# Where a fused cross-attention kernel runs its context normalisation steps and issues its loads

## The chip, the cores and the metric

One core of a Trainium2 chip. The metric is the device time of one execution in microseconds; three runs of the kernel before gave 1990.89, 1991.17 and 1993.92 us.

## The reference, cut to what matters

Cross-attention with 8 batches, 512 queries, 512 context rows, 1024 channels and 16 heads of 64 channels. Only the context is layer-normalised.

```python
a = layer_norm(ctx) * gamma + beta          # (8, 512, 1024)
Q = x @ Wq.T;  K = a @ Wk.T;  V = a @ Wv.T  # 16 heads of 64
p = softmax(where(mask, Q @ K.T * 64**-0.5, -inf))
y = x + tanh(gate) * ((p @ V) @ Wo.T)
```

## The kernel before, in words

Everything is computed on transposed tiles: 128 channels on the partitions, 512 queries or context rows along the free axis. A *body* k (0 to 63) handles one pair of heads of one batch b = k // 8, j = k % 8; the program is unrolled, and "body j" or "(b, j)" names one. "(j, h)" in the tables is body j, half h. In one body TensorE does, for each half h (one head): the scores of head h (L412, L413), the values of the head before (L432, L433), the output projection of pair k-2 (out_step, L438 to L442), and between them, dealt out by `FILL`, the 72 matmuls of the projections of pair k+1 in the order WQ, WK, WV (L485 to L489). Every operand is split into a high and a low part, so each product takes three matmuls (two for scores and values). A plain body has 132 matmuls, four of them the transposes of V (turn_v, L421).

The other engines follow their own written order; each one issues strictly in order, and semaphores join them:

- VectorE (DVE): block_maxima (L847), group_maxima (L853), key_maxima (L859), spread_maxima (L864), subtract (L869), v_low (L891), o_add (L909), column_sums (L875), accumulate (L914, the output into xy), then q_low (L897), the same chain for the other half, inverse_sums (L880 to L886), accumulate, k_low (L902), o_add and column_sums. In batch 0 norm_quarter (L968) normalises a quarter of the next context; in later batches only its statistics are taken here. o_add(k, 0) waits until GpSimd's o_scale(k-1) has read o32 (om_done). TensorE's second scores wait for both accumulates of the first half, its WK for v_low, its WV for q_low, and out_step for subtract.
- ScalarE (ACT): copy_vt (L647), o_high (L702), gather_maxima (L637) and hand_out_maxima (L642), which wait for VectorE, o_move (L681), exp (L657), v_high (L652), p_high (L662), q_high (L668, L669), which waits for the scores of its half, and k_high (L675, L676). In body 6 of a batch (kind "prepare" in batch 0, "ready" in batches 1 to 6) it also makes x_high (L714) and the eight gamma and beta steps a_float (L723) of the next context; in body 7 ("switch") a_high (L731).
- GpSimd (POOL): p_low (L1147), o_low (L1162), key_sums (L1151, L1153), o_scale (L1158); in batch 0 the splits of the weights (L1142); x_low (L1184) in body 6 and a_low (L1189) in body 7. In batches 1 to 6 it also normalises the next context, which is loaded again, transposed: `turned` (L1169 to L1179) adds the row vector of minus the means ("centre") and multiplies by the row vector of inverse deviations ("scale"), quarter by quarter. `TURNED_NORM` says in which body and half; in the first half that is ahead of o_scale and p_low(1, 0). "centre" waits for its quarter (turned_ld) and for the row vectors of its pair of quarters (row_in).
- SyncE (SP) issues all DMAs, and waits, in order. In a body of batches 1 to 6: load_kept(WV), exchange_sums (the softmax sums through HBM, L241 to L245), WQ, WK, WO, mask, store_y, the next context (load_ctx), the transposed context (load_turned, L259), spread_rows, and x. load_kept waits until TensorE has finished with the weights in place: with WQ's in the first half of a body, with WK's in the second, with WO's and WV's at its end.

spread_rows(b, pair) turns the means and inverse deviations, which stand one per partition, into row vectors: four DMAs of 128 elements of 4 bytes write them to HBM (L268), SyncE waits until all have landed, and two DMAs read them back, broadcast to all partitions (L271), into w_raw.

## Time and profile before

| | |
|---|---|
| three runs, us | 1990.89, 1991.17, 1993.92 |
| profiled execution, us | 1995.22 |
| its span, us | 1993.4 |
| granted TensorE clock, mean share | 0.996 |
| PE busy, us | 1941.4 (97%) |
| DVE busy, us | 1618.6 (81%) |
| POOL busy, us | 1573.6 (79%) |
| ACT busy, us | 1284.8 (64%) |
| DMA moved, MB | 356.67 (mean 179 GB/s) |

The profiled execution is one more run, with the profiler on. Times in the views count from the start of the span. "[2.52 <-DVE m_four L853]" behind an instruction means that its engine idled 2.52 us before it and that this instruction ended the wait; two or more of a kind in a row are merged, with their number and the time from the first's start to the last's end. A window gives its length, then for each engine the busy time and the number of instructions (PE, PEld, DVE, ACT, POOL), the share of the full TensorE clock that was granted, the share of time that the DMA engines were busy, and GB/s; its sum line adds up several windows.

### The profile page before, as it was taken

The numbers are of one execution on the slowest core, as the hardware profiler recorded it, in microseconds if no ns is written. First come the engines' busy times: TensorE is split into PE (matmuls) and PEld (weight loads), VectorE is DVE, ScalarE is ACT, GpSimd is POOL, SyncE is SP. The second block draws the span as 40 slices with busy tenths as digits, with TensorE's granted clock in tenths as the row PEclk, the third lists the DMA queues.
The fourth block names the chain that finished last, engine by engine and source line by source line (L and its number), as shares of the span: only waits on it lengthen the run. The fifth ranks groups of instructions, "written<-read, shape, count | busy, mean of one in ns | idle before, by whom it ended". The sixth has DMA issues, their size and how long they took to land.

```text
span 1993.4 us, 26143 instructions
## 1 busy us (share of the span) xinstructions
PE 1941.4 (97%) x8528; PEld 1570.1 (79%) x8528; DVE 1618.6 (81%) x2089; ACT 1284.8 (64%) x2375; POOL 1573.6 (79%) x851
## 2 busy tenths in 40 slices
PE   6999999999999999999999999999999999999997
PEld 5777778887788777888788887888778888788886
DVE  7688878887788777888788887888778888778878
ACT  5767776567656576655865668665686566756554
POOL 3899997789867888678876789768897688966664
PEclk9999999999999999999999999999999999999999
DMA  7577545664365543664446553555534655435422
GB/s 265 180 246 254 180 158 188 207 218 159 122 216 179 196 175 111 232 203 167 153 149 216 186 204 121 182 198 186 203 124 156 234 161 191 150 129 191 155 103 107
DMA packets 150039, 356.67 MB, mean 179 GB/s; under 512 B 63504, under 2 KB 67600, under 8 KB 149008
## 3 DMA queue, kind: packets, MB, share of 16 engines
q1 hardware_dynamic: 149904, 354.99, 51.4%
q8 instruction: 70, 1.15, 0.2%
q14 instruction: 65, 0.53, 0.1%
HBM read 303.54 MB, written 51.39 MB: 178 GB/s over the span
## 4 chain that ended last, share of the span: by engine, by line
PE 65%; ACT 8%; POOL 8%; DVE 7%; DMA 6%; issue 3%; SPq 2%; POOLq 0%; ACTq 0%; DVEq 0%
PE pj L485 12%; PE pj L487 12%; PE pj L489 12%; PE sc L438 4%; PE sc L442 4%; PE sc L439 4%; PE pv L432 4%; PE sc L412 4%; PE sc L413 4%; PE pv L433 4%; POOL a_lo L1189 4%; DVE mq L847 3%; DMA rows<-rstd 2%; POOL p_lo L1147 2%; ACT prob L657 2%
## 5 line engine op out<-in xcount | busy, mean ns | idle before, releaser
L1147 POOL TENSOR_TENSOR p_lo<-prob,p_hi 128x1024 fp32r<-128x1024 f32 x256 | 613.7, 2409 | 151.3 <-ACT p_hi L662 151.3
L485 PE MATMUL pj<-a_hi,w_hi 128*128 128x512 f32 x1024 | 403.9, 394 | 10.3 <-DVE qt L897 3.2
L489 PE MATMUL pj<-a_hi,w_lo 128*128 128x512 f32 x1024 | 401.4, 392 | 0.0
L487 PE MATMUL pj<-a_lo,w_hi 128*128 128x512 f32 x1024 | 401.1, 392 | 0.0
L847 DVE TRANSPOSE_TENSOR_REDUCE mq<-sc 128x32 f32<-128x1024 f32 x256 | 303.7, 1224 | 72.6 <-PE sc L413 71.7
L657 ACT ACTIVATE prob<-prob 128x1024 f32<-128x1024 f32 x256 | 271.6, 1061 | 101.2 <-DVE prob L869 100.8
L914 DVE SCALAR_TENSOR_TENSOR xy<-sc,tg_b,xy 128x1024 f32<-128x1024 f32 x244 | 304.7, 1272 | 15.0 <-PE sc L442 8.9
L869 DVE TENSOR_TENSOR prob<-sc,m_b 128x1024 f32<-128x1024 f32 x256 | 301.5, 1219 | 4.4
L1151 POOL TENSOR_TENSOR prob<-prob 128x1024 f32<-128x1024 f32 x126 | 302.5, 2401 | 0.0
L662 ACT CAST p_hi<-prob 128x1024 fp32r<-128x1024 f32 x256 | 269.3, 1052 | 3.5
L485 PEld LDWEIGHTS pj<-a_hi,w_hi 128*128 128x128 f32 x1024 | 193.1, 189 | 60.3 <-issue 6.1
L1158 POOL TENSOR_TENSOR r_b<-o,r_b 128x512 f32<-128x512 f32 x62 | 81.1, 1308 | 191.5 <-DVE r_b L886 191.5
L489 PEld LDWEIGHTS pj<-a_hi,w_lo 128*128 128x128 f32 x1024 | 193.1, 189 | 41.6
L487 PEld LDWEIGHTS pj<-a_lo,w_hi 128*128 128x128 f32 x1024 | 193.1, 189 | 40.5
L485 PE MATMUL pj<-x_hi,w_hi 128*128 128x512 f32 x512 | 208.0, 406 | 15.2 <-DVE x_lo L926 8.5
L668 ACT CAST qt<-pj 64x512 fp32r<-64x512 f32 x128 | 74.3, 580 | 220.4 <-PE sc L413 192.8
L412 PE MATMUL sc<-qt,kt 128*128 128x512 f32 x512 | 200.9, 392 | 5.5 <-DVE prob L869 3.4
L438 PE MATMUL sc<-o_hi,w_hi 128*128 128x512 f32 x494 | 197.8, 400 | 8.3 <-DVE prob L869 8.0
L432 PE MATMUL pv<-p_hi,v_st 128*128 128x512 f32 x512 | 200.5, 392 | 3.8 <-POOL p_lo L1147 3.7
L489 PE MATMUL pj<-x_hi,w_lo 128*128 128x512 f32 x512 | 202.0, 395 | 0.0
L487 PE MATMUL pj<-x_lo,w_hi 128*128 128x512 f32 x512 | 201.8, 394 | 0.0
L413 PE MATMUL sc<-qt,kt 128*128 128x512 f32 x512 | 200.1, 391 | 0.0
(129 smaller groups left out, 3735.5 us busy)
## 6 DMA issues: line engine op xcount, KB each, us to landing
w_hi<-kept_hi SPq DMA_DIRECT2D x224, 512.0 KB, 3.7
w_lo<-kept_lo SPq DMA_DIRECT2D x224, 512.0 KB, 4.7
xy<-in_xT SPq DMA_DIRECT2D x32, 512.0 KB, 6.2
cx<-in_ctx SPq DMA_DIRECT2D x32, 512.0 KB, 8.3
kept_hi<-w_hi SPq DMA_DIRECT2D x32, 512.0 KB, 5.4
kept_lo<-w_lo SPq DMA_DIRECT2D x32, 512.0 KB, 6.1
out_y<-xy SPq DMA_DIRECT2D x7, 2048.0 KB, 9.8
cx<-in_ctxT SPq DMA_DIRECT2D x24, 512.0 KB, 7.3
```

The source lines that it names most:

```text
L412: pe.matmul(sc[:, s], kt[:, h, 0, cols], qt[:, h, 0], start=True, stop=False)
L413: mm = pe.matmul(sc[:, s], kt[:, h, 1, cols], qt[:, h, 1], start=False, stop=True)
L432: pe.matmul(pv[h][:, 0], w, p_hi[:, s], start=s == 0, stop=False)
L485: pe.matmul(dst, w_hi[:, w, cols], s_hi[:, i], start=i == 0, stop=False)
L487: pe.matmul(dst, w_hi[:, w, cols], s_lo[:, i], start=False, stop=False)
L489: mm = pe.matmul(dst, w_lo[:, w, cols], s_hi[:, i], start=False, stop=i == KT - 1)
L657: act.activation(p, p, ACT.Exp, scale=SCALE).then_inc(exp_done, 1)
L847: dve.tensor_reduce(out=mq[:, 2 * i:2 * i + 2], in_=sc[:, 2 * i:2 * i + 2].rearrange("p s (b j) -> p s b j", j=32), op=ALU.max, axis=mybir ...
L869: dve.tensor_tensor(prob[:, h, 2 * i:2 * i + 2], sc[:, 2 * i:2 * i + 2], m_b[:].rearrange("p (o t) -> p o t", o=1).to_broadcast((P, 2, T)) ...
L914: dve.scalar_tensor_tensor(out=y, in0=sc[:, 2 * where:2 * where + 2], scalar=tg_b[:, bass.ds(parity, 1)], in1=y, op0=ALU.mult, op1=ALU.add ...
L1147: pool.tensor_tensor(p_lo[:, 2 * i:2 * i + 2], prob[:, h, 2 * i:2 * i + 2], f32(p_hi[:, 2 * i:2 * i + 2]), ALU.subtract).then_inc(pl_done, 1)
L1151: pool.tensor_tensor(prob[:, h, 0:2], prob[:, h, 0:2], prob[:, h, 2:4], ALU.add).then_inc(sum_done, 1)
```

## The change

- SyncE, batches 1 to 6: spread_rows of pairs 0 and 1 moves from bodies 2 and 3 to bodies 3 and 4, directly behind exchange_sums; the mask, context, transposed context and x loads move from the end of the body's list to in front of WQ's load. On GpSimd the uses of the row vectors stay where they are but for centre 3, which goes from (5, 0) to (4, 1).
- ScalarE, body 6 of batches 1 to 6: the eight a_float go from four pairs among the exponentials to three at the body's start, four between q_high(k, 0) and q_high(k, 1), and one at its end. TensorE's wait for all of them at the start of body 7 is left out in those batches (it guards PSUM banks that only batch 0's steps read).
- Bodies 0 and 1 of batch 0: v_high and v_low go ahead of the exponentials and of subtract.
- Body 5 of batch 0: norm_quarter goes from in front of key_maxima to behind subtract.

```diff
--- before.py
+++ after.py
@@ -49,8 +49,9 @@
 
 
 TURNED_LOADS = {2: 0, 3: 1}
+SPREAD_ROWS = {3: 0, 4: 1}
 TURNED_NORM = {(3, 0): (("centre", 0), ("scale", 0)), (3, 1): (("centre", 1),), (4, 0): (("scale", 1), ("centre", 2)),
-               (4, 1): (("scale", 2),), (5, 0): (("centre", 3), ("scale", 3))}
+               (4, 1): (("scale", 2), ("centre", 3)), (5, 0): (("scale", 3),)}
 
 
 FILL = ((5, 4, 7, 2, 18), (5, 4, 9, 2, 16))
@@ -334,23 +335,24 @@
                         keep_split(NUMBER[WO, PAIRS - 1])
                     load_kept(WV, (j + 1) % PAIRS, k)
                     exchange_sums(k - 1)
+                    if j in SPREAD_ROWS:
+                        spread_rows(b, SPREAD_ROWS[j])
+                    if j == 0:
+                        next_mask(b)
+                    for s in CTX_LOADS[1].get(j, ()):
+                        load_ctx(b, s)
+                    if j in TURNED_LOADS:
+                        load_turned(b, TURNED_LOADS[j])
+                    if 2 <= j <= 5:
+                        load_x(b, j - 2)
                     load_kept(WQ, (j + 2) % PAIRS, k)
                     load_kept(WK, (j + 2) % PAIRS, k)
                     if k == PAIRS + 1:
                         sp.wait_ge(w_out[WO], 32 * PAIRS)
                     if k > PAIRS:
                         load_kept(WO, (j - 1) % PAIRS, k)
-                    if j == 0:
-                        next_mask(b)
                     if j == 1:
                         store_y(b - 1, k)
-                    for s in CTX_LOADS[1].get(j, ()):
-                        load_ctx(b, s)
-                    if j in TURNED_LOADS:
-                        load_turned(b, TURNED_LOADS[j])
-                        spread_rows(b, TURNED_LOADS[j])
-                    if 2 <= j <= 5:
-                        load_x(b, j - 2)
 
             def last_batch():
                 b = B - 1
@@ -513,7 +515,7 @@
                 stream = projections(k, b, kind)
                 for h in range(2):
                     f = FILL[h]
-                    if kind == "switch" and h == 0:
+                    if kind == "switch" and h == 0 and b == 0:
                         pe.wait_ge(at_done, b * KT + 2 * KT)
                     if kind == "prepare" and h == 1:
                         pe.wait_ge(at_done, b * KT + (KT + 4))
@@ -738,11 +740,16 @@
                 if begun and splits(*out_split(k)):
                     ge(act, op_done, k * 4 - 8)
                     split_w(*out_split(k))
+                if kind == "ready":
+                    for i in range(3):
+                        a_float(b, i)
                 if kind == "switch":
                     for i in range(KT // 2):
                         a_high(k, b, i)
                 gather_maxima(k, 0)
                 hand_out_maxima(k, 0)
+                if k < 2:
+                    v_high(k)
                 if kind == "switch":
                     for i in range(KT // 2, KT):
                         a_high(k, b, i)
@@ -753,17 +760,21 @@
                 if begun:
                     o_move(k - 1, 1)
                 exp(k, 0, 0)
-                v_high(k)
+                if k >= 2:
+                    v_high(k)
                 p_high(k, 0, 0)
                 exp(k, 0, 1)
-                if kind in ("prepare", "ready"):
+                if kind == "prepare":
                     a_float(b, 0)
                     a_float(b, 1)
                 p_high(k, 0, 1)
-                if kind in ("prepare", "ready"):
+                if kind == "prepare":
                     a_float(b, 2)
                     a_float(b, 3)
                 q_high(k, 0)
+                if kind == "ready":
+                    for i in range(3, KT - 1):
+                        a_float(b, i)
                 q_high(k, 1)
                 if (j, 0) in MOMENTS[b > 0] and b < B - 1:
                     moments(b, MOMENTS[b > 0][j, 0])
@@ -782,15 +793,17 @@
                 exp(k, 1, 0)
                 k_high(k, 0)
                 p_high(k, 1, 0)
-                if kind in ("prepare", "ready"):
+                if kind == "prepare":
                     a_float(b, 4)
                     a_float(b, 5)
                 exp(k, 1, 1)
-                if kind in ("prepare", "ready"):
+                if kind == "prepare":
                     a_float(b, 6)
                     a_float(b, 7)
                 k_high(k, 1)
                 p_high(k, 1, 1)
+                if kind == "ready":
+                    a_float(b, KT - 1)
 
             def last_body(k):
                 copy_vt(k)
@@ -974,15 +987,20 @@
                 block_maxima(k, 0, 0)
                 block_maxima(k, 0, 1)
                 group_maxima(k, 0)
-                if b == 0 and (j, 0) in NORM:
+                if b == 0 and j == 6:
                     norm_quarter(NORM[j, 0])
                 key_maxima(k, 0)
                 spread_maxima(k, 0)
+                if k < 2:
+                    v_low(k)
                 subtract(k, 0, 0)
                 subtract(k, 0, 1)
+                if b == 0 and j == 5:
+                    norm_quarter(NORM[j, 0])
                 if kind == "prepare":
                     accumulate(k, 0, 0, 0, 0, b % 2)
-                v_low(k)
+                if k >= 2:
+                    v_low(k)
                 if begun:
                     o_add(k - 1, 1)
                     column_sums(k - 1, 1)
```

## Rows read from the trace of the kernel before

**Rows 1.** Page: span, and section 1 (busy us, share, instructions).

```profile
span 1993.4 us, 26143 instructions
...
PE 1941.4 (97%) x8528; PEld 1570.1 (79%) x8528; DVE 1618.6 (81%) x2089; ACT 1284.8 (64%) x2375; POOL 1573.6 (79%) x851
```

**Rows 2.** Windows of bodies 6 and 7, batch 3 (columns as said above).

```profile
952.78:983.98 31.20, 30.42 (x134) 24.06 (x132) 22.64 (x28) 25.18 (x47) 28.77 (x18) 1.00 0.45 158
983.98:1016.25 32.27, 30.94 (x132) 24.23 (x133) 25.07 (x32) 25.23 (x46) 29.32 (x18) 1.00 0.38 130
```

**Rows 3.** Windows, sums over batches 1 to 6: bodies 0-3; 4-5; 6-7.

```profile
sum 712.83, PE 712.83 PEld 583.63 DVE 609.29 ACT 429.70 POOL 510.98; mean PE 118.81 PEld 97.27 DVE 101.55 ACT 71.62 POOL 85.16
...
sum 360.99, PE 358.26 PEld 291.64 DVE 296.13 ACT 212.07 POOL 318.33; mean PE 59.71 PEld 48.61 DVE 49.36 ACT 35.35 POOL 53.05
...
sum 380.88, PE 368.02 PEld 289.75 DVE 286.25 ACT 302.46 POOL 348.43; mean PE 61.34 PEld 48.29 DVE 47.71 ACT 50.41 POOL 58.07
```

**Rows 4.** Timeline of ACT, batch 3, bodies 5 (923.09) and 6 (952.78).

```profile
940.22 0.58 ACT L668 CAST qt<-pj 64x512 fp32r<-64x512 f32 x1 [3.40 <-PE sc L413]
...
952.98 0.59 ACT L647 COPY vt<-pj 128x512 f32<-128x512 f32 x1 [0.99 <-PE pj L489]
...
956.60 0.66 ACT L637 COPY m_four<-m_four 32x16 f32<-32x16 f32 x3 [2.52 <-DVE m_four L853]
...
964.47 1.51 ACT L723 ACTIVATE cx<-cx,bet,gam 128x512 f32<-128x512 f32 x2
```

**Rows 5.** Timeline of POOL, body 7 of batch 3 (983.98).

```profile
993.48 7.58 POOL L1189 TENSOR_TENSOR a_lo<-cx,a_hi 128x512 fp32r<-128x512 f32 x6
...
1003.39 2.53 POOL L1189 TENSOR_TENSOR a_lo<-cx,a_hi 128x512 fp32r<-128x512 f32 x2
```

**Rows 6.** DMA view of 1135.5 to 1149: GB/s in 40 slices.

```profile
GB/s 401 364 316 316 376 437 376 376 449 413 401 425 425 292 113 14 0 0 0 0 0 0 0 0 0 0 0 0 0 0 0 0 0 0 0 0 0 70 55 64
```

**Rows 7.** Timeline of SP: body (3, 5) from 923.09; end of (4, 3).

```profile
935.99 1.75 SPq L245 DMA_DIRECT2D r_four<-sums  x4
...
1135.66 0.43 SPq L268 DMA_DIRECT2D rows<-rstd  x1
1146.37 0.80 SPq L271 DMA_DIRECT2D w_raw<-rows  x2
```

**Rows 8.** Line 271 (the row vectors' loads), all 24 of them.

```profile
DMA to landing us min/median/max: 3.0/4.8/6.3
```

**Rows 9.** Timeline of POOL, body 3 of batch 3 (863.01).

```profile
882.38 4.91 POOL L1179 TENSOR_TENSOR cx<-cx,w_raw 128x1024 f32<-128x1024 f32 x2
...
889.33 2.42 POOL L1147 TENSOR_TENSOR p_lo<-prob,p_hi 128x1024 fp32r<-128x1024 f32 x1
```

**Rows 10.** Timelines of PE, DVE, start of body (3, 6), 952.78.

```profile
954.59 0.39 PE L485 MATMUL pj<-x_hi,w_hi 128*128 128x512 f32 x1
...
957.54 0.39 PE L432 MATMUL pv<-p_hi,v_st 128*128 128x512 f32 x1
...
952.05 0.68 DVE L909 TENSOR_TENSOR o<-pv,o_tmp 64x512 f32<-64x512 f32 x1
...
953.88 1.25 DVE L847 TRANSPOSE_TENSOR_REDUCE mq<-sc 128x32 f32<-128x1024 f32 x1 [0.53 <-PE sc L413]
```

**Rows 11.** Batch 0: windows (body 5; a slow stretch), timelines of PE, DVE.

```profile
186.42:220.37 33.95, 31.47 (x133) 25.45 (x132) 29.75 (x38) 21.81 (x39) 30.29 (x16) 0.95 0.61 204
...
51.03:54.42 3.39, 3.39 (x9) 2.61 (x10) 0.17 (x1) 3.13 (x5) 3.24 (x2) 0.53 0.87 272
...
51.03 0.60 PE L485 MATMUL pj<-a_hi,w_hi 128*128 128x512 f32 x1 [2.05 <-DVE v_st L891]
...
70.41 0.47 PE L485 MATMUL pj<-x_hi,w_hi 128*128 128x512 f32 x1 [1.20 <-ACT vt L647]
...
196.78 0.50 PE L438 MATMUL sc<-o_hi,w_hi 128*128 128x512 f32 x1 [2.48 <-DVE prob L869]
...
190.86 3.01 DVE L968 TENSOR_SCALAR cx<-cx,nmean,rstd 128x1024 f32<-128x1024 f32 x1
```

## The prediction

> **What bounds the kernel now.** The page comes first: TensorE is busy for 97% of the span with 8528 matmuls [rows 1]. So the end can move only where TensorE waits, and I cut the span at body starts (the first score matmul of a head pair) to find those places. In batch 3 body 6 takes 31.20 us and body 7 32.27 [rows 2]. Batches 1 to 6 all behave alike: their bodies 0 to 3 sum to 712.83 us, which makes an undisturbed body 29.70; bodies 4 and 5 to 360.99, 4.6 over 12 x 29.70; bodies 6 and 7 to 380.88, 24.5 over [rows 3]. Those 29.1 us, and the waits of batch 0, are all that the change can win. Below, "at 14.7" means 14.7 us after the start of the body.
>
> **Gamma steps (a_float), batches 1 to 6.** Eight ACTIVATEs a batch, about 0.71 us each back to back, sit between the exponentials and casts of body 6 [rows 4]: they delay the q casts, then VectorE's q_low, and last the k casts, so that copy_vt of body 7 starts about 2 us late. After the change three run at body start, where ScalarE idles 2.52 us before gather_maxima: 3 x 0.71 = 2.1, cover enough. Four run after q_high(0), where a plain body idles 3.40 us before q_high(1): 2.8, covered. The last goes in front of the next copy_vt, where 0.99 us is idle [rows 4]; x_high, which stays, takes 0.6 of that, so vt comes about 0.3 late, and the first WQ matmul wants it at 1.8, a full microsecond later. Body 6 falls to 29.70: 1.50 x 6 = 9.0 us. The wait on at_done, which would hold the scores of body 7 for that last step, is gone for these batches.
>
> Body 7 doesn't fall all the way. GpSimd has six a_low, p_low, two a_low, p_low in a row [rows 5]. Started from a body 6 without the late ScalarE, I get the first a_low at 7.6 instead of 9.5, the last done at 20.05, and p_low(0,1) at 22.4. TensorE wants them at 19.6 and 22.1: 0.8 us stays. Gain 2.57 - 0.8 = 1.77, times 6 = 10.6.
>
> **Loads reordered, batches 1 to 6.** No DMA is added, only SyncE's order changes. Today spread_rows comes last in bodies 2 and 3 and blocks SyncE over the body's end; V's weights for body 4 then start late and TensorE waits for them. That is the 4.6 us of bodies 4 and 5, and it goes, since V's load now has SyncE free at the body's start. In bodies 0 to 2 the context and x loads now stand ahead of WQ's. WQ is issued some 2 us later behind at most 1.5 MB; the queue moves 512 KB in about 1.3 us (400 GB/s, [rows 6]), so it lands by 25, wanted at 31.3: nothing.
>
> **What the new order costs.** spread_rows of pair 0 moves from the end of body 2 to body 3, behind exchange_sums, yet GpSimd's first use of it, turned("centre", 0), stays in (3, 0). In a plain body SyncE is through with exchange_sums at 14.7 [rows 7]. Then:
> - Four 0.5 KB DMAs are issued to about 16.2. The trace has none in a quiet queue. In one spread the last was issued at 1135.66 and SyncE went on at 1146.37 [rows 7]; the DMA engines were already idle from 1140.9 on [rows 6]. So over 5 us of it was no queueing behind bulk loads. The four land over about 5 us. Bounds: overlapping as r_four's four are issued, in 1.75 us, done at 18; or the whole 10.7 after the last issue, done at 27. I take 16.7 for the first (2 after its issue) and 5 more: 21.7, because the idle engines show the tail to be the transfer's own.
> - The two row vectors then need 3.0 to 6.3 us, median 4.8 [rows 8], the second one issued 0.4 later: ready at 21.7 + 0.4 + 4.8 = 26.9 = x (from 18 + 0.4 + 3.0 = 21.4 to, with a second late, 29).
>
> GpSimd comes to "centre" at 19.4 today, with its row in place, takes 4.91 us for centre and scale, and starts p_low(1,0) at 26.32 [rows 9]. After the change it waits to x. Then centre, scale (4.9), o_scale (1.3), p_low(1,0) and p_low(1,1) (2.35 each) end at x + 11.0. TensorE wants the last one at 4.76 - 0.2 of the next body, so at 34.25; and VectorE's o_add waits for o_scale, done at x + 6.3 against 28.96 with 0.53 us of slack behind it [rows 10]. Both give the same threshold: a stall of x - 23.3, 3.6 us. WQ of body 4 is now issued after the spread, behind two context loads and one of x: five loads of 1.3 us make it x + 6.8 = 33.7, wanted at 31.3 [rows 10]. That 2.4 us overlaps the other stall, but after idle times of 2.05 and 2.48 us the trace shows TensorE at 1.2 instead of 2.4 GHz for a few us, which adds about 0.5 here [rows 11]. Together 4.1.
>
> Pair 1 does the same in body 4: centre 2 is the second step of (4, 0), with one turned step less behind it, so the threshold is 25.8, and x = 26.9 costs 1.1. Centre 3, moved to (4, 1), gives GpSimd four steps in body 4 and one in body 5. Its backlog is worked off in body 5 (19.4 + 2.4 of 29.7 us) before x_low: nothing. Cost 5.2 x 6 = 31.2 us.
>
> **Batch 0.** In body 5 the normalisation ran 3.01 us, started as GpSimd went from one operation to the next, with key_maxima and everything of that half behind it; TensorE waited 2.48 and then ran at half clock, and the body took 33.95 [rows 11]. Moved behind subtract it costs 1.0 to 3.0 us (I take 1.85: the rest of a GpSimd operation and its own 0.56) and pushes v_low, o_add and both accumulates, for which the second scores wait: about 0.95, and 0.5 more at out_step. 4.25 - 1.45 = 2.8 gained. In bodies 0 and 1 the early V copies end TensorE's waits for v_low, 2.05 us in body 0, but the body's end hangs on ScalarE's chain, as the 1.20 us wait for vt in body 1 shows [rows 11]. v_low ahead of subtract puts 0.7 us into that chain, q_low(0) leaves it earlier only in body 0: -1.3 and +0.4, so 1.0 gained (bounds 0 and 4).
>
> **Sum.** -9.0 - 10.6 - 4.6 - 2.8 - 1.0 = -28.0, and +31.2: +3.2 us. The profiled execution took 1995.2 (span 1993.4), 4.1 above the median 1991.2 of the runs; the difference is put onto the median: 1994.4, rounded 1994. Each microsecond of x is worth 12 us, so x decides, and with it I would be within or just beyond 0.2% (4 us), about what a measurement tells from no change.
>
> **Rivals.**
> - *The rows come early.* With an empty queue the four small DMAs overlap, and x is 21 to 26. For it: no row shows them alone. Against it: the idle 5 us [rows 6]. At x = 25 the cost is 1.7 x 6 = 10, time 1973; below 23.3 none, 1963. Chance 0.22. The Trainium skill (DMA: Bandwidth & Descriptors, "Anatomy of one DMA") gives a DMA about 2.0 us fixed, most of it the write receipt. By that rule alone the last small one would land at 18.2 and the vectors at 20.9, no stall, 1963; the trace of before doesn't agree, as its small DMAs took 10.7 us.
> - *Slower: the stall feeds itself.* Its place is the hand-over from body 3 to 4. Where x passes 27.6, WQ's wait passes 3 us, half clock follows in both bodies, and the stall of body 4 passes 1.8: 6.6 us a batch at 27.6 and 7.4 at 28, so +12 to +16 us, 2003 to 2008, and more beyond. The point from which it decides is x = 27.6. For it: the longest landings [rows 8]. Chance 0.18.
> - *The gamma steps don't free body 6* because ScalarE's start idle is too short: then 9 us less is won, 2003. Body 7's wait for a_low speaks for GpSimd as the next bound, the idle rows against. Chance 0.05, with other small errors that give no change.
>
> **Numbers.** The forecast has 0.55 with x from 26.0 to 27.6, a range of its own of 1981 to 2003, of it 0.15 faster, 0.20 same, 0.20 slower. Faster 0.15 + 0.22 = 0.37; same 0.20 + 0.03 = 0.23; slower 0.20 + 0.18 + 0.02 = 0.40. The range 1966 to 2008 leaves out the stall-free end of the first rival.
>
> **What would show it.** Right: bodies 6 at 29.7 and 7 near 30.5 in batches 1 to 6; SyncE waiting some 5 us for rows<-rstd from 16 on in bodies 3 and 4; GpSimd idle before L1179's first centre; bodies 4 (whose start takes the stall) about 34, body 5 near 31; half clock after WQ's wait. Wrong: bodies 3 to 5 all at 29.7, or body 6 still over 30.5; then the landing of the small DMAs or the idle of ScalarE was misread.

## The result and the profile after

The changed kernel takes 2043.74 us (median of 4 runs, 2042.27 to 2047.24) beside 1991.03 (median of 4) for the kernel before on the same chip: a ratio of 1.0266, interval 1.0247 to 1.0285. It is 53 us slower; the forecast was 1994 with a range up to 2008. The profiled execution took 2042.95. Page of the kernel after, span, section 1, and three groups of section 5 (busy, mean ns | idle before them, releaser):

```profile
span 2041.2 us, 26143 instructions
PE 1956.4 (96%) x8528; PEld 1583.0 (78%) x8528; DVE 1617.1 (79%) x2089; ACT 1287.7 (63%) x2375; POOL 1570.1 (77%) x851
...
L487 PE MATMUL pj<-x_hi,w_hi 128*128 128x512 f32 x512 | 214.4, 419 | 59.3 <-DMA w_lo<-kept_lo 47.4
L434 PE MATMUL pv<-p_hi,v_st 128*128 128x512 f32 x512 | 207.3, 405 | 5.8 <-POOL p_lo L1165 5.5
L1197 POOL TENSOR_TENSOR cx<-cx,w_raw 128x1024 f32<-128x1024 f32 x48 | 114.6, 2394 | 117.4 <-DMA w_raw<-rows 116.9
```

TensorE waits 59 us in front of the projections, mostly for weights from a DMA; GpSimd waits 117 us for the row vectors. Windows of the kernel after, as in [rows 3]: sums over batches 1 to 6 of bodies 0-3, 4-5 and 6-7; then bodies 3 to 7 of batch 3:

```profile
sum 712.75, PE 712.75 PEld 583.33 DVE 605.88 ACT 429.64 POOL 456.55; mean PE 118.79 PEld 97.22 DVE 100.98 ACT 71.61 POOL 76.09
...
sum 434.09, PE 384.37 PEld 306.02 DVE 299.08 ACT 213.25 POOL 369.46; mean PE 64.06 PEld 51.00 DVE 49.85 ACT 35.54 POOL 61.58
...
sum 361.15, PE 359.96 PEld 291.18 DVE 287.07 ACT 303.99 POOL 348.38; mean PE 59.99 PEld 48.53 DVE 47.85 ACT 50.66 POOL 58.06
...
877.02:906.70 29.68, 29.68 (x133) 24.30 (x132) 25.29 (x34) 17.96 (x35) 15.71 (x9) 1.00 0.27 59
906.70:944.67 37.97, 31.96 (x134) 25.66 (x132) 25.12 (x34) 17.77 (x33) 28.71 (x15) 0.91 0.52 171
944.67:978.62 33.95, 31.75 (x134) 25.09 (x133) 24.75 (x32) 17.77 (x33) 32.89 (x17) 0.95 0.62 230
978.62:1008.32 29.70, 29.70 (x134) 24.30 (x133) 23.93 (x30) 27.07 (x49) 28.34 (x18) 1.00 0.42 143
1008.32:1038.80 30.48, 30.27 (x133) 24.23 (x132) 23.89 (x31) 23.60 (x44) 29.74 (x19) 1.00 0.41 141
```

So the whole loss stands in one place: bodies 4 and 5 went from 360.99 to 434.09 (+73.1), 77.7 us over 12 x 29.70 (50.6 in bodies 4, 27.1 in bodies 5), with a lower granted clock in both. Bodies 6 and 7 went from 380.88 to 361.15 (-19.7). Batch 0 in this trace is 4.5 us shorter. How the stall comes about, timelines of the kernel after in batch 3: SP in body 3 (from 877.02), POOL and PE at the start of body 4 (906.70).

```profile
889.90 1.74 SPq L246 DMA_DIRECT2D r_four<-sums  x4
891.75 0.36 SPq L269 DMA_DIRECT2D rows<-nmean  x1
...
893.11 0.43 SPq L269 DMA_DIRECT2D rows<-rstd  x1
901.04 3.22 SPq L272 DMA_DIRECT2D w_raw<-rows  x2
904.30 0.91 SPq L260 DMA_DIRECT2D cx<-in_ctxT  x2
...
905.78 0.50 SPq L229 DMA_DIRECT2D w_hi<-kept_hi  x1
...
908.28 4.76 POOL L1197 TENSOR_TENSOR cx<-cx,w_raw 128x1024 f32<-128x1024 f32 x2 [11.85 <-DMA w_raw<-rows]
...
914.69 0.79 PE L487 MATMUL pj<-x_hi,w_hi 128*128 128x512 f32 x1 [6.01 <-DMA w_lo<-kept_lo]
915.28 0.63 PE L489 MATMUL pj<-x_lo,w_hi 128*128 128x512 f32 x1
```

SyncE issues the four small DMAs from 14.73 to 16.1 us after the body's start and can go on at 24.02: 7.9 us after the last issue. In the six batches this point lies at 23.2 to 26.2, mean 24.4. The row vectors are complete at 30.2 to 31.8, mean 30.95: that is x. WQ's weights, issued at 28.76 in this body, land at 37.63 where they are wanted at 31.3. In all six bodies 4 it is WQ's low half that ends TensorE's one long wait (5.0 to 6.5 us, mean 5.8); the rest of the 8.4 us that such a body is over 29.70 follows at its restart, with 7 to 14 matmuls at half clock. Lines 269 and 272 of the kernel after, issue to landing, in their order:

```profile
DMA to landing us min/median/max: 5.6/6.7/9.6
...
DMA to landing us min/median/max: 3.1/5.4/7.7
```

Where these 7.9 us go the DMA views show, which count the packets by size; those of the small DMAs are under 512 B. Kernel after, 893.5 to 894.3 and 894.3 to 900.7; then the kernel before in [rows 6], 1140.1 to 1141.1 and 1141.1 to 1146.3:

```profile
DMA packets 288, 0.00 MB, mean 1 GB/s; under 512 B 288, under 2 KB 288, under 8 KB 288
...
DMA packets 1, 0.01 MB, mean 1 GB/s; under 512 B 0, under 2 KB 0, under 8 KB 0
...
DMA packets 556, 0.07 MB, mean 68 GB/s; under 512 B 540, under 2 KB 540, under 8 KB 556
...
DMA packets 0, 0.00 MB, mean 0 GB/s; under 512 B 0, under 2 KB 0, under 8 KB 0
```

In the kernel after, the last small packet has run 1.1 us after the last issue, and SyncE goes on 5.9 to 8.5 us after that packet (12 spreads), in which no more of them runs. In the kernel before, most of the small packets run only at 1140.1 to 1141.1, behind the bulk loads, 4.5 us and more after the last issue (1135.66), and SyncE goes on 5.3 us after them (5.1 to 6.3 in its 12 spreads). So most of the price of a spread is the time between its last packet and its landing.

### The profile page after: what moved, and what is told of

It reads as the page before. It is cut to its first block, busy times and chain, and to the rows that moved or that the text cites. A ratio compares the mean times of both kernels' runs of the same rounds, so it can differ in the third digit from the quotient of the medians.

```text
span 2041.2 us, 26143 instructions
## 1 busy us (share of the span) xinstructions
PE 1956.4 (96%) x8528; PEld 1583.0 (78%) x8528; DVE 1617.1 (79%) x2089; ACT 1287.7 (63%) x2375; POOL 1570.1 (77%) x851
## 3 DMA queue, kind: packets, MB, share of 16 engines
q1 hardware_dynamic: 149904, 354.99, 50.6%
## 4 chain that ended last, share of the span: by engine, by line
PE 55%; POOL 12%; DMA 12%; DVE 11%; ACT 4%; SPq 3%; issue 3%; POOLq 0%; DVEq 0%; ACTq 0%
PE pj L487 10%; PE pj L489 10%; PE pj L491 10%; DMA rows<-rstd 5%; PE pv L434 4%; PE sc L440 4%; PE sc L444 4%; PE sc L441 4%; POOL a_lo L1207 3%; PE pv L435 3%; POOL p_lo L1165 3%; PE sc L414 3%; PE sc L415 3%; DVE mq L860 3%; DMA w_raw<-rows 2%
## 5 line engine op out<-in xcount | busy, mean ns | idle before, releaser
L487 PE MATMUL pj<-x_hi,w_hi 128*128 128x512 f32 x512 | 214.4, 419 | 59.3 <-DMA w_lo<-kept_lo 47.4
L434 PE MATMUL pv<-p_hi,v_st 128*128 128x512 f32 x512 | 207.3, 405 | 5.8 <-POOL p_lo L1165 5.5
L489 PE MATMUL pj<-x_lo,w_hi 128*128 128x512 f32 x512 | 206.9, 404 | 0.0
L491 PE MATMUL pj<-x_hi,w_lo 128*128 128x512 f32 x512 | 206.2, 403 | 0.0
L435 PE MATMUL pv<-p_lo,v_st 128*128 128x512 f32 x512 | 205.0, 400 | 0.0
L1197 POOL TENSOR_TENSOR cx<-cx,w_raw 128x1024 f32<-128x1024 f32 x48 | 114.6, 2394 | 117.4 <-DMA w_raw<-rows 116.9
L414 PE MATMUL sc<-qt,kt 128*128 128x512 f32 x512 | 200.5, 392 | 3.9 <-DVE prob L882 3.4
```

The source lines that it names most:

```text
L434: pe.matmul(pv[h][:, 0], w, p_hi[:, s], start=s == 0, stop=False)
L435: mm = pe.matmul(pv[h][:, 0], w, p_lo[:, s], start=False, stop=s == TB - 1)
L487: pe.matmul(dst, w_hi[:, w, cols], s_hi[:, i], start=i == 0, stop=False)
L489: pe.matmul(dst, w_hi[:, w, cols], s_lo[:, i], start=False, stop=False)
L491: mm = pe.matmul(dst, w_lo[:, w, cols], s_hi[:, i], start=False, stop=i == KT - 1)
```

## The experiments

In the expectations, *weights* means that TensorE is late because WQ's load is queued behind the spread, *vectors* that it is late because GpSimd gets the row vectors late. The forecast held that either is enough alone and that the two overlap. Edits are shown against the changed kernel unless said otherwise.

**1. WQ's load first.**

```diff
+                    load_kept(WQ, (j + 2) % PAIRS, k)
                     if j in SPREAD_ROWS:
                         spread_rows(b, SPREAD_ROWS[j])
...
-                    load_kept(WQ, (j + 2) % PAIRS, k)
```

> The changed kernel with one edit: in batches 1 to 6 SyncE issues WQ's load directly behind exchange_sums, before spread_rows. Its bodies 4 and 5 lie 77.7 us over undisturbed ones (50.6 and 27.1, summed over six batches); without that it would take 2043.7 - 77.7 = 1966. Weights theory (TensorE is late because WQ's weights are queued behind the spread): WQ lands before 31.3 us, the excess goes, about 1966. Vectors theory (GpSimd's centre waits for the row vectors, x = 31.1 us in body 3, and p_low(1,1) is late for TensorE): x grows by the 1 to 3 us that WQ's load takes ahead of it, the stall x - 23.3 is 9 to 11 us in body 4 and x - 25.8 is 6 to 8 in body 5, together 90 to 110 us: 2056 to 2076. Both sufficient, each alone (what I hold): as the vectors theory, with TensorE's wait in body 4 no longer for w_lo but for p_low.

Measured: 2064.99 us, 21 slower than the changed kernel. Its page, section 5:

```profile
L434 PE MATMUL pv<-p_hi,v_st 128*128 128x512 f32 x512 | 211.0, 412 | 75.8 <-POOL p_lo L1165 75.7
```

The wait for w_lo is gone and one for p_low of 75.7 stands in its place. The vectors alone are enough.

**2. GpSimd's steps half a body later.**

```diff
-TURNED_NORM = {(3, 0): (("centre", 0), ("scale", 0)), (3, 1): (("centre", 1),), (4, 0): (("scale", 1), ("centre", 2)),
-               (4, 1): (("scale", 2), ("centre", 3)), (5, 0): (("scale", 3),)}
+TURNED_NORM = {(3, 1): (("centre", 0), ("scale", 0), ("centre", 1)), (4, 0): (("scale", 1),),
+               (4, 1): (("centre", 2), ("scale", 2), ("centre", 3)), (5, 0): (("scale", 3),)}
```

> The changed kernel with one edit, in GpSimd's table: the steps with the row vectors of pair 0 start in the second half of body 3 (centre 0, scale 0, centre 1), scale 1 and nothing else in (4, 0), centre 2, scale 2, centre 3 in (4, 1), scale 3 in (5, 0); SyncE's order stays. Vectors theory: the excess of 77.7 us goes, about 1966. Weights theory: nothing changes in TensorE's wait for w_lo: WQ lands at 36.2 to 37.6 us where it is wanted at 31.3, a stall of 5 to 6.3 and 2 at half clock in body 4 and half as much in body 5: 2031 to 2044. What I hold (each sufficient alone) gives the same 2031 to 2044, with no wait for p_low in the bodies' first half.

Measured: 2037.89 us, 6 less. Its page, section 5:

```profile
L487 PE MATMUL pj<-x_hi,w_hi 128*128 128x512 f32 x512 | 213.4, 417 | 60.9 <-DMA w_lo<-kept_lo 48.8
```

In bodies 4 and 5 TensorE's first wait is this one, as in the changed kernel, and it is as long (48.8 us against 47.4, 12 times in both). The weights alone are enough too.

**3. Both edits.**

The diffs of 1 and 2 together.

> Both edits: WQ's load ahead of spread_rows, and GpSimd's steps with the row vectors half a body later. If weights and vectors together are the whole excess of bodies 4 and 5: 1966 (1963 to 1970), bodies 4 and 5 near 29.7 us. If a third thing holds them (GpSimd's backlog, or that WQ's late start still leaves V's weights late): a rest of 1 to 3 us a batch, 1972 to 1984, with a wait for a_low, x_low or w_lo that the trace names.

Measured: 2005.63 us. Half of the excess is gone, not all; "a third thing" was right and its size was not (40 us by the median, 30.9 in the trace, which is of the fastest execution, 1997.24; not 6 to 18). Its page, section 5:

```profile
L440 PE MATMUL sc<-o_hi,w_hi 128*128 128x512 f32 x494 | 198.7, 402 | 24.6 <-DMA w_lo<-kept_lo 22.7
```

L440 is the output projection: now WO's weights are late, the next load in SyncE's list behind its wait. Bodies 4 take 32.0 to 37.7 us, bodies 5 29.7.

**4. The queue alone** (the kernel before with SyncE's new order and GpSimd's new table).

```diff
+SPREAD_ROWS = {3: 0, 4: 1}
...
                     exchange_sums(k - 1)
+                    if j in SPREAD_ROWS:
+                        spread_rows(b, SPREAD_ROWS[j])
...
                         load_turned(b, TURNED_LOADS[j])
-                        spread_rows(b, TURNED_LOADS[j])
```

(and the loads and the table as in the change's diff.)

> The kernel before with SyncE's new order and GpSimd's new table alone; no gamma steps moved, batch 0 as before. If the parts add up: the 77.7 us of bodies 4 and 5 in place of the 4.6 that they lay over in the kernel before, 1991.2 - 4.6 + 77.7 = 2064 (2058 to 2070), that is 1.037 times the kernel before. If the moved ScalarE steps or batch 0's edits have a share in the new stall: under 2050.

Measured: 2070.56 us, 1.0393 times the kernel before (1.0377 to 1.0408). That is 0.6 us above the expected range. In its trace bodies 4 and 5 are 80.4 us over, 77.7 in the changed kernel. So the queue costs what the changed kernel shows there; a share of the other parts, which the rival put at 14 us or more, doesn't show.

**5. Everything but the queue** (SyncE's order and GpSimd's table of before), and **6. the gamma part alone.**

Run 5, against the changed kernel (and the loads back at the list's end):

```diff
-                    if j in SPREAD_ROWS:
-                        spread_rows(b, SPREAD_ROWS[j])
...
                         load_turned(b, TURNED_LOADS[j])
+                        spread_rows(b, TURNED_LOADS[j])
```

Run 6, against run 5:

```diff
-                if k < 2:
-                    v_high(k)
...
-                if b == 0 and j == 5:
-                    norm_quarter(NORM[j, 0])
```

(and both back in their old places.)

> The changed kernel with the old order of SyncE and the old table of GpSimd; gamma steps, V copies and the moved normalisation stay. Parts add up: 1991.2 - 19.6 (gamma) - 3.8 (batch 0) = 1967.8, and bodies 4 and 5 again 4.6 us over in sum: 1965 to 1970. If part of the gain at bodies 6 and 7 hung on the new queue (x and the transposed context issued earlier), a rest of 1 us or more a batch stays there: 1974 or more.

> The kernel before with the gamma part alone (ScalarE's a_float moved, TensorE's wait for them left out, batches 1 to 6). My step: 9.0 + 10.6 = 19.6 less, 1971.5 (1969 to 1974). Rival, that the left-out wait or ScalarE's late copy of V gives some of it back: over 1976. The run with the old queue less this one is batch 0's part, forecast at -3.8.

Measured: 1970.83 us (ratio to the kernel before 0.9886, 0.9869 to 0.9903) and 1974.21 (0.9894, 0.9878 to 0.991). The kernel before had a median of 1994.91 beside these two, so that the gains are 24.1 and 20.7; the terms were 23.4 and 19.6. Both times lie just above their ranges (by 0.8 and 0.2 us), which were counted from 1991.2. In both, bodies 6 take 29.70 and bodies 7 30.5. The difference of the two is batch 0's part, 3.4 us by the medians and 1.6 by the ratios. Windows of bodies 0, 1, 2, 5, 6, batch 0, of run 6 (old batch 0):

```profile
40.33:64.91 24.58, 22.54 (x102) 18.33 (x100) 14.69 (x18) 17.00 (x31) 16.69 (x9) 1.00 0.55 193
64.91:91.65 26.74, 24.55 (x110) 19.76 (x108) 19.11 (x26) 19.94 (x36) 24.02 (x12) 1.00 0.54 179
91.65:123.86 32.21, 30.47 (x133) 24.18 (x132) 26.45 (x37) 23.81 (x41) 31.59 (x16) 1.00 0.76 264
...
183.31:217.06 33.75, 31.28 (x133) 25.28 (x132) 29.65 (x38) 21.80 (x39) 30.32 (x16) 0.95 0.61 204
217.06:252.41 35.35, 33.92 (x166) 27.49 (x164) 24.97 (x32) 28.22 (x51) 35.19 (x21) 1.00 0.63 212
```

and of run 5 (new batch 0):

```profile
40.27:64.33 24.06, 22.54 (x102) 18.32 (x101) 14.40 (x18) 16.59 (x31) 16.09 (x8) 1.00 0.56 193
64.33:91.04 26.71, 24.54 (x110) 19.75 (x108) 18.86 (x26) 19.96 (x36) 23.90 (x12) 1.00 0.53 176
91.04:123.92 32.88, 30.61 (x134) 24.11 (x132) 26.43 (x37) 24.24 (x41) 32.13 (x17) 1.00 0.76 262
...
183.88:215.12 31.24, 30.50 (x133) 24.16 (x132) 28.44 (x38) 21.78 (x39) 30.35 (x16) 1.00 0.65 222
215.12:249.75 34.63, 33.94 (x165) 27.48 (x164) 24.97 (x32) 28.23 (x51) 34.47 (x21) 1.00 0.63 216
```

and of the kernel before (old batch 0), body 0:

```profile
41.08:67.24 26.16, 24.11 (x102) 19.47 (x100) 14.69 (x18) 16.98 (x31) 15.88 (x8) 0.93 0.47 156
```

The moved normalisation gives 2.5 us in body 5 (2.7 and 2.8 against the kernel before and run 4, which have the old batch 0 too). Body 6 shows no gain: the 35.35 of run 6 stands alone, the kernel before and run 4 have 34.67 and 34.65. For the early V copies one pair of traces is not enough. Bodies 0 to 2 take 83.53 us in run 6 and 83.65 in run 5, but 85.1 both in the kernel before and in run 4; the eleven kernels with the early copies lie at 83.2 to 83.7. The difference is in body 0. TensorE waits 2.0 us for v_low there in all three kernels with the old order; in two of them the granted clock then falls (0.93 over the body, 0.53 in the slow stretch of [rows 11]) and the body takes 26.2 us, in run 6 it stays at 1.00 and the body takes 24.58. So the early copies give 1.5 us where that wait is followed by half clock and nothing where it is not; what decides it no run here shows.

**7. The spread cut in two, small DMAs behind WK's load** (against run 5).

```diff
                     load_kept(WK, (j + 2) % PAIRS, k)
+                    if j in TURNED_LOADS:
+                        spread_send(b, TURNED_LOADS[j])
...
                         load_turned(b, TURNED_LOADS[j])
-                        spread_rows(b, TURNED_LOADS[j])
                     if 2 <= j <= 5:
                         load_x(b, j - 2)
+                    if j in TURNED_LOADS:
+                        spread_take(b, TURNED_LOADS[j])
```

spread_send is the part of spread_rows with the four small DMAs, spread_take the wait for them with the two loads of the row vectors.

> The kernel with the old queue (gamma and batch 0 changed) and the spread cut in two: the four small DMAs are issued right behind WK's load in bodies 2 and 3, and the wait for their landing with the two row vector loads stands at the body's end, behind x's load. No instruction is added. If it is SyncE's standing still that costs (what I hold), the 4.6 us of bodies 4 and 5 go and nothing replaces them: 1963 (1961 to 1966), the old queue's time less 4 to 5. If it is the small DMAs' place in the DMA engines that delays the loads behind them: no better than the old queue's time, and WO's or V's weights show as a new wait.

Measured: 1978.73 us, 8 more than run 5. What I held fell: SyncE stands still for the small DMAs for 49.3 us in all instead of 121.8, and it got slower. Its page, section 5, and two rows of the DMA view of 851.1 to 852 (body 2 of batch 3, 2.3 us behind the last small DMA: issue of WO's load; KB each, us to landing):

```profile
L444 PE MATMUL sc<-o_hi,w_hi 128*128 128x512 f32 x494 | 196.7, 398 | 11.9 <-DMA w_lo<-kept_lo 8.9
...
w_hi<-kept_hi SPq DMA_DIRECT2D x1, 512.0 KB, 10.5
w_lo<-kept_lo SPq DMA_DIRECT2D x1, 512.0 KB, 11.8
```

WO's load behind the small DMAs takes 9.9 to 11.2 us (high half) and 10.9 to 12.3 (low half) in all twelve such bodies; in bodies 2 of run 5, where no small DMA is ahead of it, 3.5 to 3.9 and 4.5 to 4.8. Of the load ahead of them, the low half of WK's weights, issued 0.5 us before the first small DMA, is held up in three of twelve (7.7, 12.0 and 12.2 us, otherwise 4.4 to 5.0). Bodies 3 to 5 are 12.7 us over here and 5.0 in run 5, which is the difference of the two. The small DMAs themselves hold up the bulk loads next to them.

**8. The spread cut in two, small DMAs where the changed kernel has them**, with edit 2.

```diff
                     if j in SPREAD_ROWS:
-                        spread_rows(b, SPREAD_ROWS[j])
+                        spread_send(b, SPREAD_ROWS[j])
...
                         load_kept(WO, (j - 1) % PAIRS, k)
+                    if j in SPREAD_ROWS:
+                        spread_take(b, SPREAD_ROWS[j])
```

> The changed kernel with two edits: spread_rows cut in two, its four small DMAs where they are (behind exchange_sums in bodies 3 and 4) but SyncE's wait for them and the row vector loads behind WO's load at the body's end; and GpSimd's steps half a body later. The kernel with both earlier edits still took 2005.6, with TensorE waiting for w_lo at the output projection of bodies 4 (WO's weights, issued after SyncE's 9 us wait). Theory that SyncE's standing still is the whole rest: no weights are late, 1963 to 1968. Theory that the small DMAs themselves hold up what is queued behind them: WQ's load, right behind them, lands after 31.3 and bodies 4 and 5 keep 2 us or more each, 1985 or more. The row vectors come at about 34 us; centre 0 in body 3's second half takes them at about 36, so a wait of GpSimd is the risk: each microsecond would cost up to 6.

Measured: 1998.9 us (median of 10), and the second theory is right, for bodies 4 (4.2 to 7.2 us over); bodies 5 are at most 1.4 over. SyncE now issues the context, x and WQ from 16.6 us on, right behind the small DMAs. DMA view of 876.5 to 892.5 (body 3 of batch 3; slices of 0.4 us, small DMAs issued at 876.80 to 878.15, bulk from 878.63):

```profile
GB/s 16 12 21 1 1 1 1 10 154 0 0 0 0 41 41 0 113 0 72 20 31 20 20 31 20 41 41 10 72 20 20 82 215 389 410 389 440 399 399 369
```

With bulk loads waiting from the sixth slice on, the engines move 0 to 154 GB/s for 10.7 us, 32 on average; then 400. WQ's two halves land 14.9 and 16.7 us after their issue here, at 33.9 to 35.9 us after the body's start in the six batches. The risk named was there too: the row vectors came at 40.9 to 41.8 us, not at 34, and GpSimd waited 38.2 us for them in all. But TensorE's long waits in bodies 4 and 5 are all for w_lo.

**9. Small DMAs early**: the one edit that the earlier runs point to.

```diff
                     load_kept(WV, (j + 1) % PAIRS, k)
+                    if j in SPREAD_ROWS:
+                        spread_send(b, SPREAD_ROWS[j])
                     exchange_sums(k - 1)
                     if j in SPREAD_ROWS:
-                        spread_rows(b, SPREAD_ROWS[j])
+                        spread_take(b, SPREAD_ROWS[j])
```

The wait for GpSimd (z_done) goes with spread_take.

> The changed kernel with one edit: the four small DMAs of spread_rows are issued directly behind V's load at the start of bodies 3 and 4 (from about 1.1 us on, where SyncE then idles to 11.4), and only the two row vector loads stay behind exchange_sums. Nothing is added or left out, GpSimd's table is the changed one. If the small DMAs' landing (9 us, with everything queued behind them held up) is the whole loss: they are done by about 12, the row vectors are issued at 14.7 and ready at 19 to 21.5, under the threshold of 23.3, WQ's weights land by 24; bodies 4 and 5 at 29.7 and 2043.7 - 77.7 = 1966 (1963 to 1968). If the new order of the bulk loads (context and x ahead of WQ) has a price of its own: over 1972, with a wait for w_lo. If the small DMAs still run when exchange_sums issues its own at 11.4: TensorE or VectorE waits for r_four in the first half of bodies 3 and 4, 1 us or more each.

Measured: 1965.59 us (1964.68 to 1967.4), 0.9854 times the kernel before (0.9838 to 0.9871): 29 us faster than before, 78 than the changed kernel, with the same work, and faster than run 5 too (0.9886 times the kernel before). Windows: the sum of bodies 4-5, then bodies 3 and 4 of batch 3; timelines of SP and POOL in that body 3 (from 847.45):

```profile
sum 356.38, PE 356.38 PEld 291.76 DVE 296.34 ACT 212.18 POOL 321.28; mean PE 59.40 PEld 48.63 DVE 49.39 ACT 35.36 POOL 53.55
...
847.45:877.14 29.69, 29.69 (x133) 24.32 (x132) 25.99 (x36) 17.96 (x35) 24.89 (x14) 1.00 0.57 199
877.14:906.85 29.71, 29.71 (x133) 24.31 (x132) 25.27 (x35) 17.67 (x33) 26.52 (x14) 1.00 0.58 178
...
848.58 0.38 SPq L268 DMA_DIRECT2D rows<-nmean  x1
...
860.32 1.74 SPq L246 DMA_DIRECT2D r_four<-sums  x4
862.16 0.85 SPq L275 DMA_DIRECT2D w_raw<-rows  x2
...
867.73 4.90 POOL L1202 TENSOR_TENSOR cx<-cx,w_raw 128x1024 f32<-128x1024 f32 x2 [0.86 <-DMA w_raw<-rows]
```

Nothing is over 29.71 in bodies 4 and 5. The row vectors are issued at 14.7 and ready at 20.1 here, at 19.0 to 22.7 in the twelve spreads; WQ, behind the same context and x loads as in the changed kernel, lands at 26.5 here and at 26.3 to 29.0 in bodies 3, later than the expected 24 and before the 31.3 at which it is wanted. So the new order of the bulk loads costs nothing, as the forecast had it; all of the loss is the small DMAs' landing, at a place where others hang on it.

**10. The same, issued by ScalarE** (spread_send at the start of ScalarE's bodies 3 and 4, in front of gather_maxima).

```diff
-                    if j in SPREAD_ROWS:
-                        spread_send(b, SPREAD_ROWS[j])
...
+                if 0 < b < B - 1 and j in SPREAD_ROWS:
+                    spread_send(b, SPREAD_ROWS[j])
                 if kind == "ready":
```

> As the kernel with the early small DMAs, but ScalarE issues them, in its own DMA queue, at the start of bodies 3 and 4 (in the idle time before gather_maxima), at about the time at which SyncE issues V's load. Question: does the hold-up belong to the queue in which the small DMAs stand or to the DMA engines that all queues share? Queue: V's load (issued at 0.24) lands as in other bodies, at 3.8 and 5.0 to 6.8 us. Engines: V's load of bodies 3 and 4 lands 2 us or more later than in body 2. The time itself should be 1966 (1963 to 1972) in both; four issues of some 0.4 us fit ScalarE's idle 2.5 us, otherwise bodies 3 and 4 grow by up to 1 us each.

Measured: 1965.21 us. DMA views of V's load in body 3 of batch 3, this kernel first, then the one of run 9 (where V's load goes ahead of the small DMAs):

```profile
w_hi<-kept_hi SPq DMA_DIRECT2D x1, 512.0 KB, 6.0
w_lo<-kept_lo SPq DMA_DIRECT2D x1, 512.0 KB, 9.3
```

```profile
w_hi<-kept_hi SPq DMA_DIRECT2D x1, 512.0 KB, 3.6
w_lo<-kept_lo SPq DMA_DIRECT2D x1, 512.0 KB, 4.5
```

Body 2, which the expectation named for comparison, is no good measure: its V load lands at 8.7 to 11.9 in every kernel with this order. Run 9's body 3 is a better one: in the six batches V's high half lands at 3.8 to 4.4 there and at 6.0 to 7.9 here. The small DMAs are also issued a little sooner here (the first at 0.3 us, there at 1.1), so the size of the difference is not the queue's alone. ScalarE's own queue does not shield SyncE's bulk loads. The Trainium skill says so (DMA: Bandwidth & Descriptors, "Issuing engines are not separate DMA queues": all engines' DMAs run on the same 16 DMA engines and interleave); this trace agrees. Here it cost nothing, since V's weights have time.

**11. Each small DMA twice.**

```diff
                         sp.dma_start(rows[c, s].rearrange("(p o) -> p o", o=1), one[:, s:s + 1]).then_inc(row_out, 16)
-                sp.wait_ge(row_out, n * 64 + 64)
+                        sp.dma_start(rows[2 + c, s].rearrange("(p o) -> p o", o=1), one[:, s:s + 1]).then_inc(row_out, 16)
+                sp.wait_ge(row_out, n * 128 + 128)
```

> The changed kernel with the suspected cost doubled: each small DMA of spread_rows is followed by a second one like it into another DRAM row, so eight instead of four are waited for. If they land one after the other at 1 to 1.6 us each behind a first of 5.8 (what I hold, from landings at 20.6, 21.6, 22.2, 24.0): the last lands 4 to 6 us later and x grows by as much; each microsecond of x costs two stalls of a microsecond in each of six batches, 12 us: +50 to +75, 2094 to 2119. If the 9 us are a fixed latency that overlaps: x grows only by four issues of 0.45 = 1.8, +22, 2066.

**12. Half as many, with two elements per partition.**

```diff
-                for s in (2 * pair, 2 * pair + 1):
-                    for c, one in enumerate((nmean, rstd)):
-                        sp.dma_start(rows[c, s].rearrange("(p o) -> p o", o=1), one[:, s:s + 1]).then_inc(row_out, 16)
-                sp.wait_ge(row_out, n * 64 + 64)
+                for c, one in enumerate((nmean, rstd)):
+                    sp.dma_start(rows[c, 2 * pair:2 * pair + 2].rearrange("s p -> p s"),
+                                 one[:, 2 * pair:2 * pair + 2],
...
+                sp.wait_ge(row_out, n * 32 + 32)
```

> The changed kernel with the same elements in half the DMAs: spread_rows sends its 512 elements of 4 bytes in two DMAs of 128 x 2 instead of four of 128 x 1. If each DMA has its price: landing 2 to 3 us earlier, x shorter by as much plus 0.9 of issue, 24 to 47 us less: 1997 to 2020. If each element of 4 bytes has it: only the two issues are saved (0.9 us, -11): 2033.

Measured: 2069.75 and 2047.81 us. What I held of run 11 fell: +26 by the medians and +21 by the ratios (1.0370 against 1.0266), not +50, and close to the 22 of a latency that overlaps. SyncE goes on at 27.4 instead of 24.4 (means of bodies 3), and the last of eight DMAs is issued 1.9 us later than the last of four: the other 1.0 us is not issue. In run 12 two DMAs take as long as four (24.5, the first landing at 22.5 instead of 20.6), and neither of its theories gave the time. Two, four or eight, in bodies 3 the wait ends 7.1 to 10.4 us after the last issue. So it is mostly a latency, and what is added to it goes rather by the elements (512 in two DMAs as in four, 1024 in eight) than by the DMAs: with two, the last issue is 1.3 us earlier and nothing is won. No run separates the two further. In run 11 x is 1.85 us later (32.80), and bodies 4 and 5 are 21.0 us longer in the two traces, so that a microsecond of x costs 11.4 us; by the medians it would be 14 (the traced execution of run 11, 2064.07 us, is its fastest).

## Why the prediction was wrong

- **Gamma steps: right.** -19.6 forecast, -19.7 in bodies 6 and 7 of the trace, 20.7 in run 6. Bodies 6 fell to 29.70, bodies 7 to 30.5, both as forecast.
- **Batch 0: right.** -2.8 forecast and -2.5 to -2.8 measured in body 5. The 1.0 for the V copies lies between what the traces show, nothing in one comparison and 1.5 in two; the 1.5 is half clock behind TensorE's wait in body 0, which that term didn't have.
- **Loads reordered: right.** The 4.6 us of bodies 4 and 5 go once the spread is out of the way, and WQ's load behind 1.5 MB costs nothing (run 9; in bodies 2 of the kernel after it lands by 25.9, where 25 was forecast).
- **The step that failed: "the four land over about 5 us", the first 2 after its issue, so 21.7, and then 0.4 + 4.8 for the row vectors, x = 26.9.** Measured in body 3: the first lands at 20.6, the last at 23.1 to 26.2, mean 24.4; the row vectors take 6.5 from there; x = 30.95. So 2.7 of the missing 4.05 us are the small DMAs' landing and 1.35 the row vectors' loads. I had read rightly in [rows 6, 7] that the idle stretch was the transfer's own and no queueing: all small packets had run before it. But I let it begin at a first landing "2 after its issue", for which there was no row. Counted from the last packet (1.1 us behind the last issue) the 5.3 us of that row give 22.6, and in the kernel after this last part is longer too, 5.9 to 8.0 us in bodies 3. Why, no run shows.
- **The range of x was too narrow for its own bounds.** The landing was bounded by 18 and 27, and the measured 24.4 lies within. But 27 + 0.4 + 3.0 to 6.3 is 30.4 to 33.7, and the sum stops at 29. x lay beyond 29 in all six batches, and the range of the time ended at 2008, the price of x = 28.
- **The sum of the formulas held, partly by luck.** x - 23.3 = 7.7 against 8.4 measured in bodies 4 (50.6 / 6), x - 25.8 = 5.2 against 4.5 in bodies 5 (27.1 / 6); WQ at x + 6.8 = 37.9 against 37.6 in batch 3, where x is 31.1. But the forecast put the stall of body 4 down to the vectors, with WQ's wait inside it and 0.5 us of half clock. Measured, WQ's wait comes first (5.8 us) and 2.6 follow at its restart, mostly at half clock; p_low, about as late, hides behind them. Run 1 brings it out. "12 us for each microsecond of x" is 11.4 in run 11. By that price the 4 us in x are 48 of the 50 us between forecast and result; the trace has 46.5 (77.7 against 31.2), the rest is less than what executions of the kernel before differ by (1988.9 to 1995.2). That both stalls had to go together is what runs 1 and 2 show.
- **The rival "the stall feeds itself"** met its condition: x beyond 27.6 and half clock in both bodies (granted clock 0.91 and 0.95 in batch 3). But its prices, 6.6 and 7.4 us a batch, are what x - 23.3 + 0.5 and x - 25.8 give without any feeding, and none is to be seen: pair 1's small DMAs are issued 6.8 to 8.4 us later in their body than pair 0's, always less than that body's own stall, and with this stall taken off its row vectors come at 29.4, not later than pair 0's 30.95. What the rival had right is a large x. It had 0.18, because the landing was too short.
- **The rival "the rows come early"** has no support: no small DMA of the spread landed under 3.9 us where a landing is recorded. The Trainium skill's 2.0 us fixed (DMA: Bandwidth & Descriptors, "Anatomy of one DMA") is given there for DMAs that GpSimd issues, which the prediction left out; it does not hold for these, 128 elements of 4 bytes from 128 partitions to HBM, issued by SyncE: 5.6 us at least in the kernel after.
- **Not in the prediction:** that loads queued behind the small DMAs are held up with them (runs 7, 8), and that WO's weights are the next in line behind WQ's (run 3).

## What to carry to other kernels

A step that writes columns of small elements to HBM and waits for them had a price here of 7 to 11 us from its last issue on, with two, four or eight DMAs, and it slowed the bulk loads beside it too. Look for a stretch in which its queue has nothing to do, issue it there, and wait for it only where its result is read: here that one move was worth 78 us. And where a row shows such a wait behind a bulk transfer, ask when its own packets ran, count the rest from the last of them, and carry both bounds through to the time, above all when every microsecond of it is paid in several places.

## What the runs showed of the hardware

- Small DMAs (128 elements of 4 bytes, SBUF to HBM) landed 5.6 / 6.7 / 9.6 us after issue (min, median, max) in a queue with nothing else, and 4.2 / 7.9 / 11.0 beside V's load in run 9. Their packets had all run 1.1 us after the last issue, 5.9 to 8.5 us before SyncE could go on (kernel after).
- It is not every small write to HBM: the 16 KB of the softmax sums, 128 bytes from each of 128 partitions, landed after 1.4 us in the median in the kernel before. That the 4-byte elements are the reason is likely and not shown; no run changes their size.

```profile
sums<-rq SPq DMA_DIRECT2D x63, 16.0 KB, 1.4
```

- While they were under way, a queue with over 2 MB in it moved 32 GB/s on average for some 10 us (run 8); a 512 KB load issued 2.3 us behind the last of them took 9.9 to 11.2 us, and one issued 0.5 us ahead of the first took 12 in two of twelve cases (run 7). Why the engines stand still meanwhile no run here shows.
- A second engine's queue did not shield the loads from that (run 10).
- The same idle time of 2.0 us of TensorE, at the same place in body 0, was followed by a granted clock of 0.53 over 3.4 us in the kernel before, by a body at 0.93 in run 4 as well, and by full clock in run 6.
